# Turning layer-norm rows back to feature-major on VectorE and ScalarE instead of TensorE

## The chip, the cores and the metric

One core of a Trainium2 chip runs the whole program. The metric is the device time of one execution in microseconds; a change is judged by the ratio of the two kernels' times.

## The reference

For each of B = 8 samples `x` is 512 tokens by 256 features. Two residual blocks follow one another:

```python
# block 1, "context"
ctx = causal_ema(x, tau_ctx)
gated = x * sigmoid(concat(x, ctx) @ Wg.T + bg)
h1 = gelu(x @ Wn1.T + bn1); mod = 0.5 + sigmoid(h1 @ Wn2.T + bn2)      # D = 8 channels
temporal = sum_d softmax(blend)[d] * causal_ema(gated * mod[d], tau[d])
gate = sigmoid(temporal @ Wtemp.T + btemp); soma = gelu(x @ Wsoma.T + bsoma)
out = (soma * gate) @ Wout.T
x2 = x + (out - mean(out)) / sqrt(var(out) + 1e-5) * gamma + beta     # over the 256 features
# block 2, "experts": three shared FFNs and two that the sample's type picks, 256 -> 1024 (relu) -> 256
out = x2 + g0 * (wa * expert_a(x2) + wb * expert_b(x2)) + g1 * s0(x2) + g2 * s1(x2) + g3 * s2(x2)
```

The four gates `g` are a softmax made from the FFNs' outputs at token 0.

## The kernel before

Everything but the layer norm is held feature-major: partition = feature (two tiles of 128, index `c`), free = 512 tokens. To keep fp32 precision each operand is split into a rounded "hi" part (ScalarE) and a remainder "lo" (VectorE), and each product is three fp32r matmuls.

The expert pass of sample `b` is 40 slots (`SLOTS`): five FFNs of eight 128-wide hidden tiles. In slot `k` TensorE does `up` for hidden tile `k + 2` (LAG = 2), six matmuls into one of four banks `ps_up`, then `down` for tile `k`, six matmuls that accumulate into the two banks `ps_down`. ScalarE makes `hid_hi` by a relu (L1065), VectorE `hid_lo` (L1306, `relu_lo`); TensorE's down waits for both. When an FFN's eight tiles are done, ScalarE copies `ps_down` to `y` (`read_out`, L1078), and the first down of the next FFN waits for it at L723. In each engine's own program `read_out` of FFN 3 stands at slot 32, ahead of that slot's relu:

```python
def mixture(b, k, parity, last):          # ScalarE
    if k % TPF == 0 and 0 < k < SLOTS:
        read_out(b, k // TPF - 1, parity)
    if k + LAG < (LAST_SLOTS if last else SLOTS):
        relu(b, k + LAG, last)
```

While the experts of sample `b` run, the context block of sample `n = b + 1` is computed beside them ("context period" n, n = 1 to 7; sample 0's is an opening of its own). Which step of it stands where is written out by hand: a plan for each engine maps a slot to step names. A whole-numbered slot's steps are issued before that slot's expert work, those of a half-numbered one behind it. `PLANS` holds for n = 3 to 7, `FIRST_PLANS` for n = 1, where the FFN weights are split as well, and `SECOND_PLANS` for n = 2: the same plan one slot later from slot 20 on (VectorE from 11.5 on). Each engine runs its list strictly in order; a semaphore wait holds all that is behind it.

The steps around the change, with their slots in `PLANS`: TensorE `out` (28.5) multiplies token tiles, so that the result has tokens on the partitions, in `ps_aux`; VectorE `ln_stats` (29); ScalarE `ln_sqrt` (29.5); VectorE `ln_norm` (30) writes `normed` (128 tokens x 256 features, four token tiles, L1485); TensorE `turn` (32) transposes it back, eight 128x128 transposes into `ps_aux` (L848); ScalarE `turn` (33) applies gamma and beta on the way out (L1143); VectorE `x2` (33.5) adds x (L1494); `x2_hi` (34.5), `x2_lo` (35) split it for the next sample's up products, which begin at slot 38. In slot 31 VectorE also has the gate part of sample b, one L1341 and five L1344 behind its `relu_lo`. In the period n = 2 the turn is at 33 (TensorE) and 34 (ScalarE).

Of the kernel before, what the change touches and what calls it, by code (L numbers as in the profile page):

```python
# [7 lines left out]
ALU = mybir.AluOpType  # L8
ACT = mybir.ActivationFunctionType
# [24 lines left out]
TT = T // P  # L34
# [11 lines left out]

PLAN_TENSOR = {
    0.5: ["mod_hidden"], 1.5: ["soma"], 2.5: ["mod", "gate_hidden"], 4.5: ["wgate"],
    25.5: ["tgate"], 28.5: ["out"], 32: ["turn"],
}  # L50
PLAN_SCALAR = {
    1: ["mod_hidden", "gate_part_hi"], 2: ["soma"], 3: ["mod"], 4: ["gate_exp"], 5.5: ["wgate"],
    24.5: ["temp_hi"], 26: ["tgate"], 27: ["sg_hi"], 29.5: ["ln_sqrt"], 33: ["turn"], 34.5: ["x2_hi"],
    36: ["next_x_hi"],
}
PLAN_VECTOR = {
    0.5: ["gate_part"], 1.5: ["mod_hidden_lo"], 2: ["gate_part_lo"], 3.5: ["gate_logits"],
    4.5: ["gate_soft", "mix1"], 5: ["wgate_scan"], 5.5: ["mix2", "mix3"], 6: ["gated"], 6.5: ["mix0"],
    24.5: ["temp_lo"], 26.5: ["sg"], 27: ["sg_lo"], 29: ["ln_stats"], 30: ["ln_norm"], 33.5: ["x2"], 35: ["x2_lo"],
    36.5: ["next_x_lo"],  # L60
}
for _d in range(D):
# [8 lines left out]
def from_slot(plan, first, head):  # L71
# [99 lines left out]
def build(nc, x, w_ctx, params, types_row, types_all, shared_wi, shared_wo, expert_wi, expert_wo,  # L171
# [6 lines left out]
    with ExitStack() as ctx:  # L178
# [3 lines left out]
        def sem(name):  # L182
            return ctx.enter_context(nc.semaphore(name))
# [18 lines left out]
        x2 = sb("x2", [P, 2, CT, T])  # L202
# [19 lines left out]
        soma = sb("soma", [P, CT, T])  # L222
        gates = sb("gates", [P, CT, T])
# [5 lines left out]
        normed = sb("normed", [P, TT, E])  # L229
        ident = sb("ident", [P, P])  # L230
# [56 lines left out]
        aux_ready = sems("aux_ready", 2)  # L287
# [133 lines left out]
        def col(c, i=0):  # L421
            return par[:, c + i:c + i + 1]
# [232 lines left out]
        def _(pe):  # L655
# [122 lines left out]
            def beside(step, k, p):  # L778
# [45 lines left out]
                elif step == "out":  # L824

                    pe.wait_ge(sg_hi_ready, n)
                    places = [(t, c, slice(t * P, (t + 1) * P), slice(W_OUT + c * E, W_OUT + (c + 1) * E))
                              for t in range(TT) for c in range(CT)]
                    for t, c, tok, at in places:
                        if t % 2 == 0 and c == 0 and later(p.aux[t // 2]["out"]):  # L830
                            pe.wait_ge(aux_free[t // 2], p.aux[t // 2]["out"])
                        place = ps_aux[t // 2][:, (t % 2) * E:(t % 2 + 1) * E]
                        pe.matmul(place, xg_hi[:, c, tok], wc_hi[:, at], start=t % 2 == 0 and c == 0, stop=False)  # L833
                        pe.matmul(place, xg_hi[:, c, tok], wc_lo[:, at], start=False, stop=False)  # L834
                    pe.wait_ge(sg_split, n)
# [189 lines left out]
        def _(act):  # L1025
# [72 lines left out]
            def beside(step, k, p):  # L1098
# [35 lines left out]
                elif step == "ln_sqrt":  # L1134
                    act.wait_ge(meanvar_ready, n)
                    act.activation(std[:, :], meanvar[:, :, 1], ACT.Sqrt, bias=eps[:, :]).then_inc(std_ready, 1)
                elif step == "turn":

                    if later((n - 1) * 16):
                        act.wait_ge(out_stored, (n - 1) * 16)  # L1140
                    for c in range(CT):
                        act.wait_ge(aux_ready[c], p.aux[c]["turn"] + 1)
                        act.activation(x2[:, p.n_parity, c, :], ps_aux[c][:, :], ACT.Identity, bias=col(C_BETA, c),  # L1143
                                       scale=col(C_GAMMA, c)).then_inc(aux_free[c], 1)
                elif step == "x2_hi":
                    act.wait_ge(x2_ready, n * 2 + 2)
                    hi(both(x2_hi[:, p.n_parity, :, :]), both(x2[:, p.n_parity, :, :])).then_inc(x2_hi_ready, 1)
# [147 lines left out]
        def _(dve):  # L1295
# [124 lines left out]
            def beside(step, k, p):  # L1420
# [59 lines left out]
                elif step == "ln_norm":  # L1480
# [384 lines left out]
```

## Time and profile before

| | |
|---|---|
| runs | median 1045.18 us, 1044.25 to 1045.28, three runs |
| profiled execution | span 1044.1 us from the first to the last instruction; no other time of its own is given |
| TensorE busy | 1036.7 us (99%) |
| VectorE busy | 756.8 us (72%) |
| ScalarE busy | 405.0 us (39%) |
| GpSimd busy | 16.3 us (2%) |

Read it so: with TensorE at 99%, what counts is what its queue holds and whether it ever has to wait; the other engines' shares say how much room there is on average, not whether an instruction comes in time.

### The profile page before, as it was taken

The page shows a single profiled execution, that of the slowest core. Times are in us where ns is not written, and L with a number is a line of the kernel's source. Part 1 is how long each engine was busy: PE and PEld are TensorE (multiplying, and loading weights), DVE is VectorE, ACT ScalarE, POOL GpSimd, SP SyncE. Part 2 cuts the span into 40 slices and gives each one's busy share as a digit, 9 for nine tenths or more (in the row PEclk, how much of TensorE's full clock was granted, in tenths as well). Part 3 has the DMA queues.
Part 4 walks back from the last instruction along what each step waited for, and adds up shares of the span by engine and source line. Part 5 has one row for each costly group of instructions (what it writes and reads, how often), then busy time and mean ns, then how long its engine had stood idle before and what let it go on. Part 6 is the DMA issues. An engine that isn't in the chain of part 4 may idle for free.

```text
span 1044.1 us, 12751 instructions
## 1 busy us (share of the span) xinstructions
PE 1036.7 (99%) x4850; PEld 861.1 (82%) x4850; DVE 756.8 (72%) x1260; ACT 405.0 (39%) x663; POOL 16.3 (2%) x26
## 2 busy tenths in 40 slices
PE   8999999999999999999999999999999999999998
PEld 5688888888888888888888888888888888888898
DVE  6989977799547986389764996559955599545236
ACT  8654555423443234422344223433334432423232
POOL 1200000000000000000000000000000000000000
PEclk9999999999999999999999999999999999999999
DMA  5388999786354754466544664546645465355582
GB/s 213 121 313 275 312 356 356 282 324 240 131 192 167 257 181 162 162 238 210 197 164 163 231 235 152 185 162 242 208 154 201 163 235 204 146 201 191 203 323 90
DMA packets 38302, 223.02 MB, mean 214 GB/s; under 512 B 4514, under 2 KB 5282, under 8 KB 16610
## 3 DMA queue, kind: packets, MB, share of 16 engines
q1 hardware_dynamic: 35938, 209.63, 56.1%
q0 software_dynamic: 2304, 12.58, 3.2%
q8 instruction: 38, 0.62, 0.2%
q14 instruction: 22, 0.18, 0.0%
HBM read 188.51 MB, written 33.69 MB: 213 GB/s over the span
## 4 chain that ended last, share of the span: by engine, by line
PE 96%; DMA 2%; DVE 2%; issue 0%; SPq 0%; ACT 0%; DVEq 0%
PE ps_up L665 14%; PE ps_up L695 14%; PE ps_up L696 14%; PE ps_down L737 14%; PE ps_down L741 14%; PE ps_down L738 14%; PE ps_aux L658 2%; PE ps_aux L659 2%; PE ps_aux L660 2%; DMA wi<-split_wi 1%; DVE y L1633 1%; PE ps_aux L837 1%; PE ps_aux L834 1%; PE ps_aux L833 1%; PE ps_aux L822 1%; PE ps_aux L818 1%
## 5 line engine op out<-in xcount | busy, mean ns | idle before, releaser
L1065 ACT ACTIVATE hid_hi<-ps_up 128x512 fp32r<-128x512 f32 (+1 forms) x336 | 193.5, 576 | 507.8 <-PE ps_up L665 507.6
L1306 DVE SCALAR_TENSOR_TENSOR hid_lo<-ps_up,hid_hi 128x512 fp32r<-128x512 f32 (+1 forms) x336 | 220.1, 658 | 228.9 <-ACT hid_hi L1065 227.5
L695 PE MATMUL ps_up<-x_hi_all,wi 128*128 128x512 f32 (+1 forms) x660 | 250.8, 382 | 0.4 <-DMA wi<-split_wi 0.4
L696 PE MATMUL ps_up<-x_hi_all,wi 128*128 128x512 f32 (+1 forms) x660 | 249.9, 380 | 0.0
L737 PE MATMUL ps_down<-hid_hi,wo 128*128 128x512 f32 (+1 forms) x640 | 245.3, 384 | 0.1
L738 PE MATMUL ps_down<-hid_hi,wo 128*128 128x512 f32 (+1 forms) x640 | 245.1, 384 | 0.0
L665 PE MATMUL ps_up<-x_lo_all,wi 128*128 128x512 f32 (+1 forms) x660 | 197.4, 380 | 0.2 <-DVE x_lo_all L1297 0.2
L741 PE MATMUL ps_down<-hid_lo,wo 128*128 128x512 f32 (+1 forms) x640 | 193.9, 384 | 0.0
L695 PEld LDWEIGHTS ps_up<-x_hi_all,wi 128*128 128x128 f32 x660 | 124.1, 188 | 24.1 <-DMA wi<-split_wi 0.8
L696 PEld LDWEIGHTS ps_up<-x_hi_all,wi 128*128 128x128 f32 x660 | 124.1, 188 | 23.0
L665 PEld LDWEIGHTS ps_up<-x_lo_all,wi 128*128 128x128 f32 x660 | 122.0, 188 | 24.3 <-DVE x_lo_all L1297 0.4
L737 PEld LDWEIGHTS ps_down<-hid_hi,wo 128*128 128x128 f32 x640 | 120.2, 188 | 24.7 <-issue 0.2
L738 PEld LDWEIGHTS ps_down<-hid_hi,wo 128*128 128x128 f32 x640 | 120.2, 188 | 23.5
L741 PEld LDWEIGHTS ps_down<-hid_lo,wo 128*128 128x128 f32 x640 | 119.0, 188 | 24.0 <-DVE hid_lo L1306 0.3
L1416 DVE TENSOR_TENSOR_SCAN trace<-alpha,trace 128x512 f32<-128x512 f32 x98 | 119.1, 1216 | 0.0
L1450 DVE SCALAR_TENSOR_TENSOR trace<-modb,blend_w,gates 128x512 f32<-128x512 f32 x98 | 68.9, 744 | 0.0
L1459 DVE TENSOR_TENSOR temporal<-trace,temporal 128x512 f32<-128x512 f32 x98 | 62.1, 676 | 0.0
L1373 DVE SCALAR_TENSOR_TENSOR x<-y,g,x 128x512 f32<-128x512 f32 x56 | 38.9, 746 | 0.2
L658 PE MATMUL ps_aux<-xg_hi_all,wc_hi 128*128 128x512 f32 x88 | 34.5, 392 | 0.0
L659 PE MATMUL ps_aux<-xg_lo_all,wc_hi 128*128 128x512 f32 x88 | 34.3, 389 | 0.0
L660 PE MATMUL ps_aux<-xg_hi_all,wc_lo 128*128 128x512 f32 x88 | 34.2, 389 | 0.0
L1078 ACT ACTIVATE y<-ps_down 128x512 f32<-128x512 f32 x48 | 26.1, 596 | 18.5 <-PE ps_down L741 18.5
(248 smaller groups left out, 855.1 us busy)
## 6 DMA issues: line engine op xcount, KB each, us to landing
wi<-split_wi SPq DMA_DIRECT2D x70, 1024.0 KB, 4.8
wo<-split_wo SPq DMA_DIRECT2D x70, 1024.0 KB, 4.9
modb<-mod_scratch SPq DMA_DIRECT2D x28, 512.0 KB, 4.6
split_wi<-wi SPq DMA_DIRECT2D x10, 1024.0 KB, 7.3
split_wo<-wo SPq DMA_DIRECT2D x10, 1024.0 KB, 7.6
xt<-in_x SPq DMA_DIRECT2D x8, 512.0 KB, 5.8
split_wi<-ex POOLq DMA_DIRECT2D x4, 1024.0 KB, 8.6
split_wo<-ex POOLq DMA_DIRECT2D x4, 1024.0 KB, 6.0
```

The source lines that it names most:

```text
L658: pe.matmul(ps, w_hi, x_hi, start=start, stop=False)
L665: mm = pe.matmul(ps, w_hi[c], x2_lo[:, parity, c, tokens], start=False, stop=c == CT - 1)
L695: pe.matmul(ps, w_hi, x2_hi[:, parity, c, tokens], start=c == 0, stop=False)
L696: pe.matmul(ps, w_lo, x2_hi[:, parity, c, tokens], start=False, stop=False)
L737: pe.matmul(bank, w_hi[:, cols], hid_hi[:, at % NU, tokens], start=start, stop=False)
L738: pe.matmul(bank, w_lo[:, cols], hid_hi[:, at % NU, tokens], start=False, stop=False)
L741: mm = pe.matmul(bank, w, hid_lo[:, at % NU, tokens], start=False, stop=stop)
L1065: act.activation(hid_hi[:, k % NU, tokens], ps_up[k % NU][:, tokens], ACT.Relu).then_inc(hid_hi_ready, 1)
L1306: dve.scalar_tensor_tensor(hid_lo[:, k % NU, tokens], ps_up[k % NU][:, tokens], 0.0, f32(hid_hi[:, k % NU, tokens]), ALU.max, ALU.subtract ...
L1416: scan = dve.tensor_tensor_scan(trace_of(d)[:, c, :], alpha[:, d:d + 1].broadcast_to([P, T]), trace_of(d)[:, c, :], 0.0, ALU.mult, ALU.add)
L1450: dve.scalar_tensor_tensor(trace_of(d)[:, c, :], modb[:, d // 2 % 2, d % 2, :], blend_w[:, c, d:d + 1], gates[:, c, :], ALU.mult, ALU.mult ...
L1459: dve.tensor_tensor(temporal[:, c, :], trace[:, c, :], temporal[:, c, :], ALU.add).then_inc(ema_sum, 1)
```

## The change

`normed` is turned back without TensorE. VectorE's new step `turn` transposes each 32x32 block in place in the 128x256 tile (four instructions) into `gates`. A block's rows and columns are then right, but it may lie in the wrong partition quarter. ScalarE moves the blocks: step `turn<b>`, b = 0 to 3, has four copies of 32 partitions x 256 elements from quarter a of `gates` to quarter b of `soma`. Residual and beta are put into `x2` by ScalarE beforehand (`base`, slot 20.5), and VectorE's `x2` step multiplies by gamma and adds.

```diff
 PLAN_TENSOR:  ... 28.5: ["out"]
-    32: ["turn"]
 PLAN_SCALAR:
-    33: ["turn"]
+    20.5: ["base"], 31: ["turn0"], 31.5: ["turn1"], 32.5: ["turn2"], 33: ["turn3"]
 PLAN_VECTOR:
+    30.5: ["turn"]
 FIRST_PLANS:
-    "tensor": 33.5: ["turn"];  "scalar": 34.5: ["turn"]
+    "scalar": 21.5: ["base"], 32.5: ["turn0"], 33: ["turn1"], 33.5: ["turn2"], 34.5: ["turn3"];  "vector": 32: ["turn"]
...
+        turned_in_place = gates[:, :, :].rearrange("p c t -> p (c t)").rearrange("p (t c b j) -> p b c t j", t=TT, c=CT, b=4)
+        turned = soma[:, :, :].rearrange("p c (t a j) -> p a c t j", t=TT, a=4)
...
-                elif step == "turn":                                    # TensorE
-                    pe.wait_ge(normed_ready, n)
-                    for c in range(CT):
-                        for t in range(TT):
-                            mm = pe.transpose(ps_aux[c][:, t * P:(t + 1) * P], normed[:, t, c * P:(c + 1) * P], ident[:, :])
-                        mm.then_inc(aux_ready[c], 1)
...
-                elif step == "turn":                                    # ScalarE
+                elif step == "base":
                     if later((n - 1) * 16):
                         act.wait_ge(out_stored, (n - 1) * 16)
                     for c in range(CT):
-                        act.wait_ge(aux_ready[c], p.aux[c]["turn"] + 1)
-                        act.activation(x2[:, p.n_parity, c, :], ps_aux[c][:, :], ACT.Identity, bias=col(C_BETA, c),
-                                       scale=col(C_GAMMA, c)).then_inc(aux_free[c], 1)
+                        act.activation(x2[:, p.n_parity, c, :], x_of(n)[:, c, :], ACT.Identity, bias=col(C_BETA, c))\
+                            .then_inc(base_ready, 1)
+                elif step.startswith("turn"):
+                    b = int(step[-1])
+                    act.wait_ge(blocks_turned, n * TT)
+                    for a in range(4):
+                        hi(turned[quarter(b), a], turned_in_place[quarter(a), b]).then_inc(quarter_moved, 1)
...
+                elif step == "turn":                                    # VectorE
+                    dve.wait_ge(sg_split, n)
+                    for t in range(TT):
+                        dve.wait_ge(aux_free[t // 2], p.aux[t // 2]["out"] + 1)
+                        dve.transpose(gates[:, t // 2, (t % 2) * E:(t % 2 + 1) * E], normed[:, t, :]).then_inc(blocks_turned, 1)
                 elif step == "x2":
+                    dve.wait_ge(quarter_moved, n * 16)
+                    dve.wait_ge(base_ready, n * CT)
                     for c in range(CT):
-                        dve.wait_ge(aux_free[c], p.aux[c]["turn"] + 1)
-                        dve.tensor_tensor(x2[:, p.n_parity, c, :], x2[:, p.n_parity, c, :], x_of(n)[:, c, :], ALU.add)
+                        dve.scalar_tensor_tensor(x2[:, p.n_parity, c, :], soma[:, c, :], col(C_GAMMA, c),
+                                                 x2[:, p.n_parity, c, :], ALU.mult, ALU.add).then_inc(x2_ready, 1)
```

## Rows read from the trace of the kernel before

**Rows 1.** The page: busy time by engine; the chain that ended last

```profile
PE 1036.7 (99%) x4850; PEld 861.1 (82%) x4850; DVE 756.8 (72%) x1260; ACT 405.0 (39%) x663; POOL 16.3 (2%) x26
...
PE 96%; DMA 2%; DVE 2%; issue 0%; SPq 0%; ACT 0%; DVEq 0%
```

**Rows 2.** Groups by line and shape: busy us, mean ns | idle before

```profile
L1485 DVE TENSOR_SCALAR normed<-ps_aux,meanvar,rstd 128x256 f32<-128x256 f32 x28 | 13.3, 537 | 0.3
...
L1143 ACT ACTIVATE x<-ps_aux,par 128x512 f32<-128x512 f32 x14 | 10.1, 778 | 0.0
...
L1078 ACT ACTIVATE y<-ps_down,wa_now 128x512 f32<-128x512 f32 x14 | 8.9, 685 | 4.8 <-PE ps_down L741 4.8
...
L848 PE MATMUL ps_aux<-ident,normed 128*128 128x128 f32 x56 | 7.3, 272 | 0.0
...
L1224 ACT ACTIVATE modb<-ps_aux,gw 128x256 f32<-128x256 f32 x16 | 6.3, 528 | 0.0
...
L1027 ACT ACTIVATE modh_hi<-modh 128x512 fp32r<-128x512 f32 x7 | 4.4, 633 | 0.2
L1118 ACT ACTIVATE normed<-normed 8x512 f32<-8x512 f32 x7 | 4.4, 631 | 0.2
...
L871 PEld LDWEIGHTS ps_down<-ones_r 128*128 128x128 f32 x18 | 3.9, 331 | 1.3 <-DVE ones_r L1553 1.3
...
L893 PEld LDWEIGHTS ps_down<-y,gw 128*128 128x128 f32 x16 | 3.0, 190 | 3.9 <-issue 3.6 <-ACT gw L1190 0.2
...
L1027 ACT ACTIVATE ct_hi<-gpart 128x256 fp32r<-128x256 f32 x7 | 2.8, 403 | 1.7 <-DVE gpart L1506 1.7
```

**Rows 3.** Timeline of TensorE, slots 31 to 33, period n = 7: start, length

```profile
905.06 0.39 PE L695 MATMUL ps_up<-x_hi_all,wi 128*128 128x512 f32 x1
...
907.78 1.03 PE L848 MATMUL ps_aux<-ident,normed 128*128 128x128 f32 x8
908.57 0.48 PE L695 MATMUL ps_up<-x_hi_all,wi 128*128 128x512 f32 x1
...
910.03 0.39 PE L737 MATMUL ps_down<-hid_hi,wo 128*128 128x512 f32 x1
...
911.39 0.39 PE L695 MATMUL ps_up<-x_hi_all,wi 128*128 128x512 f32 x1
```

**Rows 4.** Timeline of ScalarE, the read of FFN 3, period n = 7

```profile
907.98 1.27 ACT L1078 ACTIVATE y<-ps_down,wa_now 128x512 f32<-128x512 f32 x2 [0.77 <-PE ps_down L741]
```

**Rows 5.** Timeline of VectorE, slots 30 and 31, period n = 7

```profile
903.63 1.90 DVE L1485 TENSOR_SCALAR normed<-ps_aux,meanvar,rstd 128x256 f32<-128x256 f32 x4
905.68 0.69 DVE L1306 SCALAR_TENSOR_TENSOR hid_lo<-ps_up,hid_hi 128x512 fp32r<-128x512 f32 x1
907.25 0.69 DVE L1306 SCALAR_TENSOR_TENSOR hid_lo<-ps_up,hid_hi 128x512 fp32r<-128x512 f32 x1 [0.88 <-ACT hid_hi L1065]
907.86 0.34 DVE L1341 TENSOR_SCALAR gpart<-gw,y 128x256 f32<-128x256 f32 x1
```

**Rows 6.** Timeline of ScalarE, a 128x256 copy and its follower

```profile
181.99 0.40 ACT L1027 ACTIVATE ct_hi<-gpart 128x256 fp32r<-128x256 f32 x1
182.29 0.58 ACT L1065 ACTIVATE hid_hi<-ps_up 128x512 fp32r<-128x512 f32 x1
```

**Rows 7.** Timeline of ScalarE at slot 21, period n = 7

```profile
873.80 0.60 ACT L1065 ACTIVATE hid_hi<-ps_up 128x512 fp32r<-128x512 f32 x1 [2.12 <-PE ps_up L665]
```

**Rows 8.** Timeline, period n = 2: TensorE's down(32), VectorE behind the gate part

```profile
281.00 0.39 PE L737 MATMUL ps_down<-hid_hi,wo 128*128 128x512 f32 x1
...
283.73 0.68 DVE L1306 SCALAR_TENSOR_TENSOR hid_lo<-ps_up,hid_hi 128x512 fp32r<-128x512 f32 x1
```

**Rows 9.** Timeline, period n = 1: VectorE's norm, TensorE's down(35)

```profile
155.40 1.90 DVE L1485 TENSOR_SCALAR normed<-ps_aux,meanvar,rstd 128x256 f32<-128x256 f32 x4
...
163.82 0.39 PE L737 MATMUL ps_down<-hid_hi,wo 128*128 128x512 f32 x1
```

**Rows 10.** Windows: length, PE, PEld, DVE, ACT, POOL busy, clock, DMA share, GB/s

```profile
0.00:3.00 3.00, 1.70 (x8) 1.70 (x9) 0.39 (x7) 1.34 (x2) 0.20 (x4) 1.00 0.20 34
```

More of the change, by code:

```diff
@@ L48 @@
     0.5: ["mod_hidden"], 1.5: ["soma"], 2.5: ["mod", "gate_hidden"], 4.5: ["wgate"],
-    25.5: ["tgate"], 28.5: ["out"], 32: ["turn"],
+    25.5: ["tgate"], 28.5: ["out"],
 }
@@ L52 @@
     1: ["mod_hidden", "gate_part_hi"], 2: ["soma"], 3: ["mod"], 4: ["gate_exp"], 5.5: ["wgate"],
-    24.5: ["temp_hi"], 26: ["tgate"], 27: ["sg_hi"], 29.5: ["ln_sqrt"], 33: ["turn"], 34.5: ["x2_hi"],
+    20.5: ["base"], 24.5: ["temp_hi"], 26: ["tgate"], 27: ["sg_hi"], 29.5: ["ln_sqrt"], 31: ["turn0"], 31.5: ["turn1"], 32.5: ["turn2"],
+    33: ["turn3"], 34.5: ["x2_hi"],
     36: ["next_x_hi"],
@@ L58 @@
     4.5: ["gate_soft", "mix1"], 5: ["wgate_scan"], 5.5: ["mix2", "mix3"], 6: ["gated"], 6.5: ["mix0"],
-    24.5: ["temp_lo"], 26.5: ["sg"], 27: ["sg_lo"], 29: ["ln_stats"], 30: ["ln_norm"], 33.5: ["x2"], 35: ["x2_lo"],
+    24.5: ["temp_lo"], 26.5: ["sg"], 27: ["sg_lo"], 29: ["ln_stats"], 30: ["ln_norm"], 30.5: ["turn"], 33.5: ["x2"], 35: ["x2_lo"],
     36.5: ["next_x_lo"],
@@ L79 @@
     "sync": from_slot(PLAN_SYNC, 8, {1: ["mod"], 1.5: ["modb0", "modb1"]}),
-    "tensor": {0.5: ["mod"], 1.5: ["wgate"], 27.5: ["tgate"], 30: ["out"], 33.5: ["turn"]},
-    "scalar": {0.5: ["mod"], 2: ["wgate"], 26: ["temp_hi"], 28: ["tgate"], 29: ["sg_hi"],
-               31: ["ln_sqrt"], 34.5: ["turn"], 35.5: ["x2_hi"], 37: ["next_x_hi"]},
+    "tensor": {0.5: ["mod"], 1.5: ["wgate"], 27.5: ["tgate"], 30: ["out"]},
+    "scalar": {0.5: ["mod"], 2: ["wgate"], 21.5: ["base"], 26: ["temp_hi"], 28: ["tgate"], 29: ["sg_hi"],
+               31: ["ln_sqrt"], 32.5: ["turn0"], 33: ["turn1"], 33.5: ["turn2"], 34.5: ["turn3"], 35.5: ["x2_hi"], 37: ["next_x_hi"]},
     "vector": {2: ["wgate_scan", "gated"],
-               26: ["temp_lo"], 28.5: ["sg"], 29: ["sg_lo"], 30.5: ["ln_stats"], 31.5: ["ln_norm"], 35: ["x2"], 36: ["x2_lo"],
+               26: ["temp_lo"], 28.5: ["sg"], 29: ["sg_lo"], 30.5: ["ln_stats"], 31.5: ["ln_norm"], 32: ["turn"], 35: ["x2"], 36: ["x2_lo"],
                37.5: ["next_x_lo"]},
@@ L313, in build @@
         rstd_ready = sem("rstd_ready")
-        normed_ready = sem("normed_ready")
-        turned_ready = sem("turned_ready")
+        blocks_turned = sem("blocks_turned")
+        base_ready = sem("base_ready")
+        quarter_moved = sem("quarter_moved")
         x2_ready = sem("x2_ready")
@@ L409, in build, with quarter @@
         open_total_of = open_traces[3]
+        turned_in_place = gates[:, :, :].rearrange("p c t -> p (c t)").rearrange("p (t c b j) -> p b c t j", t=TT, c=CT, b=4)
+        turned = soma[:, :, :].rearrange("p c (t a j) -> p a c t j", t=TT, a=4)
         def x_of(n):
             return xt[n % 2][:, :, :]
+        def quarter(i):
+            return slice(i * P // 4, (i + 1) * P // 4)
         def raw_part(i):
@@ L840, in beside @@
                             mm.then_inc(aux_ready[t // 2], 1)
-                elif step == "turn":
-                    pe.wait_ge(normed_ready, n)
-                    for c in range(CT):
-                        if later(p.aux[c]["turn"]):
-                            pe.wait_ge(aux_free[c], p.aux[c]["turn"])
-                        for t in range(TT):
-                            mm = pe.transpose(ps_aux[c][:, t * P:(t + 1) * P], normed[:, t, c * P:(c + 1) * P], ident[:, :])
-                        mm.then_inc(aux_ready[c], 1)
                 elif step == "gate_hidden":
@@ L1488, in beside @@
                             last.then_inc(aux_free[t // 2], 1)
-                    dve.wait_ge(aux_free[1], p.aux[1]["out"] + 1)
-                    dve.nop().then_inc(normed_ready, 1)
+                elif step == "turn":
[3 more added lines that the diff above has]
+                        dve.transpose(gates[:, t // 2, (t % 2) * E:(t % 2 + 1) * E], normed[:, t, :]).then_inc(blocks_turned, 1)
                 elif step == "x2":
+                    dve.wait_ge(quarter_moved, n * 16)
+                    dve.wait_ge(base_ready, n * CT)
                     for c in range(CT):
-                        dve.wait_ge(aux_free[c], p.aux[c]["turn"] + 1)
-                        dve.tensor_tensor(x2[:, p.n_parity, c, :], x2[:, p.n_parity, c, :], x_of(n)[:, c, :], ALU.add)\
-                            .then_inc(x2_ready, 1)
+                        dve.scalar_tensor_tensor(x2[:, p.n_parity, c, :], soma[:, c, :], col(C_GAMMA, c),
+                                                 x2[:, p.n_parity, c, :], ALU.mult, ALU.add).then_inc(x2_ready, 1)
                 elif step == "x2_lo":
```

## The prediction

> **What bounds the kernel.** I read the page first: TensorE is busy 99% of the span and holds 96% of the chain that ended last [rows 1]. A microsecond taken off TensorE's queue is therefore a microsecond off the end, and one in which it stands still is added. Then the grouped rows of the instructions that the change touches [rows 2], and the timelines of the three engines at the place of the change. The profiled span is 1044.1 us; the runs' median, 1045.18, is 1.1 us more, which I take as what lies around the span and leave alone.
>
> A slot of the expert pass is one "up" product (six matmuls) and one "down" product (six), 2.72 us. In the seventh context period slot 31 opens at 905.06, the eight transposes start at 907.78, slot 32's up at 908.57 and its down at 910.03 [rows 3]. What bounds slot 32's down is more than its weights: it opens the fifth FFN, and L723 makes it wait until ScalarE has read the fourth FFN out of the same bank (y, L1078). In the profile this is just in time: that read runs from 907.98 [rows 4], done for the first bank near 908.66, for the second near 909.25.
>
> **What the change takes off TensorE.** From slot 31's start, 905.06, to slot 32's start, 908.57, is 3.51 us, 0.79 over the 2.72 of a plain slot; from there to the slot after (911.39) is 2.82, 0.10 over it [rows 3]. Eight transposes cost 0.89 us, in seven periods 6.2 us. The 273 ns of one matmul times 56 would give 15 us, but they overlap [rows 2], so the spacing counts. If nothing else happened the time would be 1045.2 - 6.2 = 1039.0.
>
> **What it adds elsewhere.** VectorE: four 128x256 block transposes per period. No row shows one. Cheapest neighbour: a tensor_scalar of this shape in SBUF, 0.34 us; dearest: the one that writes normed, 537 ns, four in 1.90 us, so 454 ns apart [rows 2, 5]. Back-to-back VectorE instructions start some 75 ns before the last ends (0.69 long, the next 0.61 behind it [rows 5]), so 0.27 apart at the low end. I take 0.35 apart and 0.42 for the last, between the ends: four in 1.47 us (low 1.15, high 1.89).
> ScalarE: sixteen copies of 32 partitions x 256 elements. Nearest row: the 128x256 copy in SBUF, 403 ns on average; where a relu follows at once, it starts 0.30 later [rows 2, 6]. That a quarter of the partitions makes a copy cheaper isn't to be expected: a copy of 512 elements takes 0.63 us on 8 partitions and on 128 [rows 2]. I take 0.31 apart (low 0.30, high 0.40, no overlap). The Trainium skill (ScalarE: Activation LUTs, What ACT_TABLE_LOAD costs) gives 186 ns + 0.833 ns an element, with 93 ns of overlap; by it a copy is 0.40 and 0.306 apart, and the sum would stay.
> "base" is two activations at slot 20.5, at most as long as the two that go away at slot 33 (0.78 [rows 2]), in a ScalarE that rests 2.12 us between relus there [rows 7]: nothing.  The x2 step takes 0.75 instead of 0.68 twice, on VectorE, nothing: its consumer, TensorE at slot 38, is some 8 us later. No DMA is moved.
>
> **Where it lands.** This is the step that decides. Both engines take their work in the order in which the plan lists it. ScalarE's order in the third to seventh period is: relu(32); turn0 (waits for all four transposes, four copies); relu(33); turn1 (four copies); then, at slot 32, the read of the fourth FFN; relu(34); turn2; turn3. So that read, for which TensorE waits, now stands behind the wait for VectorE and eight copies.
> Seventh period: VectorE finishes the norm at 905.53 and has relu_lo(32) at 905.68, after which the next can start at 906.29 [rows 5]. Transposes end at 906.29 + 1.47 = 907.76. ScalarE, with 0.04 for the semaphore: 907.80 + 8 x 0.31 + 0.50 (relu(33) in series) = 910.78, where the read begins; its first bank is ready 0.68 later (685 ns [rows 2]), 911.46. TensorE would want it at 910.03 - 0.89 = 909.14. Wait 2.32, and 0.13 more because the second bank comes 0.58 after the first while TensorE wants it 0.45 after: 2.45. Less the 0.89, the period loses 1.56 us. The offsets from the norm to TensorE's transposes are the same in periods three to seven (4.15 us from 903.63 to 907.78 here), so 5 x 1.56 = 7.8. Low: 5 x 1.16 = 5.8. High (transposes to 908.18, read from 911.92): 5 x 2.70 = 13.5.
> Second period: its plan is one slot later from 11.5 (VectorE) and 20 (ScalarE) on, so only turn0 stands ahead of the read, but the transposes, at 31.5, stand behind slot 31's gate part: VectorE is at relu_lo(33), a 0.34 and five gate products until 283.73, where the transposes can start [rows 8]. They end at 285.20; turn0 4 x 0.31, the read's first bank 0.68: 287.16. TensorE starts slot 32's down at 281.00 in the profile, its transposes come a slot later, so nothing has been saved yet: wait 6.16 + 0.13 = 6.29, loss 5.40 (low 5.04, high 6.18).
> First period: its turn0 comes at 32.5, after the read, so no read is held. What is queued behind the copies is relu(35): the norm ends at 157.30 [rows 9], transposes 158.77, eight copies and a relu 161.9; TensorE's down(35) wants it at 163.82 - 0.89 = 162.9. In time. relu(36), behind a splitting round, turn2: 164.6 against 165.65. Gain 0.89, at the high costs nothing (0.1 and then 0.5 late, and the copies' other followers).
> Sum: -0.9 + 5.4 + 7.8 = +12.3 us (low 10.0, high 19.7).
> After the waits nothing else is late: in periods three to seven turn3 ends near 915, x2 and its halves are ready by 920, and slot 38 isn't before 925. relu_lo(33) and the gate part slide behind the late relu(33) to about 913.5, and relu_lo(34) is wanted after 917.
>
> **The clock.** The granted TensorE clock is 1.00 (2.4 GHz) even in the first 3 us, which hold the longest idle stretch of TensorE, 1.3 us [rows 2, 10]. Yet after its idle start the first 18 weight loads (fp32) take 331 ns against 190 for later ones of that type, 2.5 us lost in all [rows 2, 10]. A 6.3 us wait may cost that again: 0 to 2.6, I take 1.3. So +13.6: 1044.1 + 13.6 = 1057.7 in the span, **1058.8 us** by the runs. The Trainium skill (TensorE: Matmul & The Clock Gate, Why this matters for your kernels) says that a long idle gap between matmuls sends the array back to half clock; the granted clock here has not yet shown it.
> The same skill's VectorE: DVE Perf Modes (Rules for kernel authors) says to give a 128x128 transpose to TensorE where PSUM will do as its destination, and by its table the VectorE one is the shorter (311 against 390 ns). Here neither figure decides; the queue does.
>
> **Rivals.**
> Only the saving shows (1039.0): the quarter copies would have to be so cheap that the read isn't late: it must start by 908.42, which leaves 1.6 us for four transposes and eight copies after 906.29; a copy's time doesn't fall with its partitions, by the rows above. And with copies at nothing the second period still waits for the transposes until 284.9 at best, 4.7 us with the read: -6.2 + 4.7 = -1.5, 1043.7, no change that could be told. So below 1043 is possible only if TensorE doesn't wait for that read. Chances 2% faster, 2% for 1043.7.
> Each wait costs the clock: 2.6 us at all six instead of 1.3 at one, 1073. For: the opening's slow loads. Against: a wait of 2.4 us isn't one of 6, and the granted clock at the slow loads is 1.00 too, so that they may have another cause [rows 10]. The skill's rule above would be this one, if 2.4 us counted as long. 9%.
> Both operations dearer: transposes at twice 0.454 = 0.91 apart, copies at 0.53 (the 128x256 activation out of PSUM at L1224 [rows 2], no overlap): the period waits 906.29 + 3.6 + 0.04 + 4.2 + 0.5 + 0.7 - 909.14 = 6.2, loss 5.4, times 5 = 27; the second 8.4; the first some 3: 1084. For: no row has either operation, both read or write in runs of 32 elements. 7%.
>
> **Numbers.** The sum as worked out has 80%, its own range 1055 to 1067.5 (10.0; 19.7 + 2.6). For 8 in 10 I take 1054 to 1070. What a measurement of this kernel can tell from no change is 0.2%, 2.1 us. Faster 2%, same 2%, slower 96%.
>
> **What would show it.** ScalarE's L1078 after "turn1" by about 2.8 us in periods three to seven, TensorE idle before L737 of slot 32, released by y, 2 to 3.5 us five times and about 6 us once, none in the first; the four block transposes near 0.42 us and the sixteen copies near 0.40. I'm wrong if L1078 isn't waited for, if the transposes are done long before 907.8, or if the copies on 32 partitions are far from 0.3 apart.

## The result and the profile after

The changed kernel takes 1081.17 us (1080.19 to 1081.94, four runs) against 1045.03 (1044.25 to 1045.28, four runs): ratio 1.0344, 95% interval [1.0329, 1.0358]. The direction was forecast, the size was not: 36 us slower, where I gave 14 and a range up to 25.

The page, busy time by engine, the chain that ended last, and two groups (answering to [rows 1]):

```profile
PE 1044.7 (97%) x4794; PEld 862.5 (80%) x4794; DVE 765.8 (71%) x1288; ACT 449.8 (42%) x775; POOL 16.3 (2%) x26
...
PE 89%; DVE 3%; ACT 3%; DMA 2%; issue 2%; SPq 0%; POOL 0%; DVEq 0%; POOLq 0%; ACTq 0%
...
L745 PE MATMUL ps_down<-hid_hi,wo 128*128 128x512 f32 (+1 forms) x640 | 248.3, 389 | 23.0 <-ACT y L1077 21.5
...
L1026 ACT ACTIVATE soma<-gates 32x256 f32<-32x256 f32 x112 | 46.4, 414 | 24.6 <-DVE gates L1497 22.1
```

TensorE has 56 instructions less and is busy 8 us longer. ScalarE waits 22.1 us for the block transposes, and TensorE 21.5 us for ScalarE's read-out of `ps_down` (L1077 now, L1078 before). The view of who waited for whom, TensorE alone (us in total, times, longest):

```profile
PE ps_down L745 <- ACT y L1077: 21.5, 6, 6.4
PE ps_aux L666 <- ACT modh L1109: 3.9, 1, 3.9
...
PE ps_down L745 <- DVE y L1330: 0.9, 1, 0.9
...
PE ps_down L745 <- ACT hid_hi L1064: 0.6, 1, 0.6
```

Six waits for the read, one in each of the periods 2 to 7, as forecast. The other three lie in the first period, and none of them was there before. Waits explain some 27 us; the rest is slow work behind them, shown next. The seventh period, timelines of ScalarE, VectorE and TensorE (start, length), answering to [rows 3 to 5]:

```profile
938.26 1.74 ACT L1026 ACTIVATE soma<-gates 32x256 f32<-32x256 f32 x4 [3.00 <-DVE gates L1497]
939.90 0.57 ACT L1064 ACTIVATE hid_hi<-ps_up 128x512 fp32r<-128x512 f32 x1
940.50 1.73 ACT L1026 ACTIVATE soma<-gates 32x256 f32<-32x256 f32 x4
942.25 1.27 ACT L1077 ACTIVATE y<-ps_down,wa_now 128x512 f32<-128x512 f32 x2
```

```profile
936.21 0.68 DVE L1310 SCALAR_TENSOR_TENSOR hid_lo<-ps_up,hid_hi 128x512 fp32r<-128x512 f32 x1
936.81 1.42 DVE L1497 STREAM_TRANSPOSE gates<-normed 128x256 f32<-128x256 f32 x4
```

```profile
939.45 0.61 PE L673 MATMUL ps_up<-x_lo_all,wi 128*128 128x512 f32 x2
943.08 0.47 PE L745 MATMUL ps_down<-hid_hi,wo 128*128 128x512 f32 x1 [3.02 <-ACT y L1077]
...
945.40 0.63 PE L703 MATMUL ps_up<-x_hi_all,wi 128*128 128x512 f32 x1
...
947.55 0.40 PE L745 MATMUL ps_down<-hid_hi,wo 128*128 128x512 f32 x1
```

The order on ScalarE is the one of the prediction: wait for the transposes, four copies, a relu, four copies, and only then the read. Slot 32's down starts at 943.08; a start-to-start spacing of 0.23 behind the up product's last matmul would have been 939.90: 3.18 us lost. Then down and the next up take 2.32 and 2.15 us instead of 1.36 each. The windows say why (length, busy time of PE, PEld, DVE, ACT, POOL, granted clock, DMA share, GB/s):

```profile
938.00:941.00 3.00, 2.06 (x10) 1.37 (x8) 0.72 (x2) 2.62 (x7) 0.00 (x0) 1.00 0.38 117
941.00:944.00 3.00, 0.92 (x3) 0.73 (x4) 2.82 (x7) 2.93 (x6) 0.00 (x0) 0.94 0.55 232
944.00:947.00 3.00, 3.00 (x8) 2.33 (x8) 0.73 (x2) 2.83 (x8) 0.00 (x0) 0.50 0.00 0
947.00:950.00 3.00, 3.00 (x14) 2.41 (x14) 1.62 (x3) 1.08 (x3) 0.00 (x0) 0.99 0.37 101
```

After the wait the granted clock is 0.50 (1.2 instead of 2.4 GHz) for some 3.4 us: eight matmuls in 3 us instead of fourteen. That costs 0.96 in the down product, 0.79 in the up product and 0.03 behind them, 1.78 us. 3.18 + 1.78 - 0.89 saved = 4.07, and the period is 4.0 longer.

The second period, VectorE, ScalarE and TensorE, answering to [rows 8]:

```profile
290.81 1.42 DVE L1497 STREAM_TRANSPOSE gates<-normed 128x256 f32<-128x256 f32 x4
```

```profile
292.27 1.73 ACT L1026 ACTIVATE soma<-gates 32x256 f32<-32x256 f32 x4 [5.87 <-DVE gates L1497]
294.02 1.26 ACT L1077 ACTIVATE y<-ps_down,wa_now 128x512 f32<-128x512 f32 x2
```

```profile
294.85 0.76 PE L745 MATMUL ps_down<-hid_hi,wo 128*128 128x512 f32 x1 [6.37 <-ACT y L1077]
```

The first period, ScalarE, GpSimd and TensorE, answering to [rows 9]; behind them two windows:

```profile
158.06 3.50 ACT L1026 ACTIVATE soma<-gates 32x256 f32<-32x256 f32 x8 [1.20 <-DVE gates L1497]
161.58 0.60 ACT L1064 ACTIVATE hid_hi<-ps_up 128x512 fp32r<-128x512 f32 x1
...
185.05 1.06 ACT L1026 ACTIVATE ex<-ex 128x1024 fp32r<-128x1024 f32 x1 [6.96 <-DMA ex<-in_expert_wo]
186.13 1.28 ACT L1109 ACT_TABLE_LOAD   x1
187.42 0.69 ACT L1109 ACTIVATE modh<-ps_aux,par 128x512 f32<-128x512 f32 x1
```

```profile
165.87 0.54 POOL L1785 DMA_DIRECT2D split_wi<-ex  x1 [14.41 <-DVE ex L1301]
...
177.95 0.53 POOL L1777 DMA_DIRECT2D ex<-in_expert_wo  x1 [9.00 <-DMA split_wi<-ex]
```

```profile
165.79 0.47 PE L745 MATMUL ps_down<-hid_hi,wo 128*128 128x512 f32 x1 [0.56 <-ACT hid_hi L1064]
178.40 0.47 PE L745 MATMUL ps_down<-hid_hi,wo 128*128 128x512 f32 x1 [0.94 <-DVE y L1330]
188.16 0.50 PE L666 MATMUL ps_aux<-xg_hi_all,wc_hi 128*128 128x512 f32 x1 [3.92 <-ACT modh L1109]
```

```profile
185.00:188.00 3.00, 0.00 (x0) 0.00 (x0) 0.00 (x0) 2.92 (x3) 0.00 (x0) 1.00 0.97 397
188.00:191.00 3.00, 2.84 (x9) 2.28 (x10) 1.41 (x2) 2.97 (x6) 0.00 (x0) 0.72 0.15 61
```

In this pass the expert weights are split as well, a tile at a time: GpSimd loads a tile, ScalarE and VectorE split it, GpSimd stores it and loads the next into its place. The eight copies put relu(35) at 161.58, where it was at 157.68 before; VectorE's remainder of the tile stands behind relu_lo(35) and came 3.9 us later (163.95 instead of 160.05). The store went out at 165.87 instead of 161.98, into a stretch (170 to 182) in which the transfers fill 0.97 to 1.00 of the DMA engines, as they do at the same place before, and the next tile's load at 177.95 instead of 170.62. ScalarE asks for that tile at slot 40 and stands 7 us before it, with the next period's Gelu behind it, and TensorE 3.9 us for the Gelu, with the clock down after it. An operation that is 4 us late came back as a hole 25 us later. (The times of before are its own timelines' starts of the same instructions. The changed kernel's opening is 0.6 us shorter, so against the start of the period each of them is 0.6 later still.)

The whole difference by periods, measured from the start of one period's reciprocal of the norm to the next one's, so that each length holds one turn:

| kernel | period 1 | 2 | 3 to 6, each | 7 to the end |
|---|---|---|---|---|
| before | 122.81 | 122.93 | 125.62 | 140.7 |
| after | 130.74 | 130.35 | 129.63 | 144.8 |
| difference | +7.9 | +7.4 | +4.0 | +4.1 |

7.9 + 7.4 + 4 x 4.0 + 4.1 = 35.4; the opening was 0.6 shorter; the spans differ by 34.9 (1079.0 to 1044.1).

### The profile page after: what moved, and what is told of

It is laid out like the page before. It is cut to its first block, busy times and chain, and to the rows that moved or that the text cites. A ratio compares the mean times of both kernels' runs of the same rounds, so it can differ in the third digit from the quotient of the medians.

```text
span 1079.0 us, 12773 instructions
## 1 busy us (share of the span) xinstructions
PE 1044.7 (97%) x4794; PEld 862.5 (80%) x4794; DVE 765.8 (71%) x1288; ACT 449.8 (42%) x775; POOL 16.3 (2%) x26
## 4 chain that ended last, share of the span: by engine, by line
PE 89%; DVE 3%; ACT 3%; DMA 2%; issue 2%; SPq 0%; POOL 0%; DVEq 0%; POOLq 0%; ACTq 0%
PE ps_down L745 13%; PE ps_up L703 13%; PE ps_up L704 13%; PE ps_down L749 13%; PE ps_down L746 13%; PE ps_up L673 13%; PE ps_aux L666 2%; PE ps_aux L668 2%; PE ps_aux L667 2%; ACT soma L1026 2%; DMA wi<-split_wi 1%; DVE y L1641 1%; DMA ex<-in_expert_wo 1%; PE ps_aux L842 1%; PE ps_aux L845 1%
## 5 line engine op out<-in xcount | busy, mean ns | idle before, releaser
L745 PE MATMUL ps_down<-hid_hi,wo 128*128 128x512 f32 (+1 forms) x640 | 248.3, 389 | 23.0 <-ACT y L1077 21.5
L746 PE MATMUL ps_down<-hid_hi,wo 128*128 128x512 f32 (+1 forms) x640 | 247.7, 388 | 0.0
L749 PE MATMUL ps_down<-hid_lo,wo 128*128 128x512 f32 (+1 forms) x640 | 196.8, 389 | 0.0
L703 PEld LDWEIGHTS ps_up<-x_hi_all,wi 128*128 128x128 f32 x660 | 126.0, 191 | 25.6 <-DMA wi<-split_wi 1.1
L704 PEld LDWEIGHTS ps_up<-x_hi_all,wi 128*128 128x128 f32 x660 | 126.0, 191 | 23.8
L1026 ACT ACTIVATE soma<-gates 32x256 f32<-32x256 f32 x112 | 46.4, 414 | 24.6 <-DVE gates L1497 22.1
L667 PE MATMUL ps_aux<-xg_lo_all,wc_hi 128*128 128x512 f32 x88 | 34.9, 397 | 0.0
## 6 DMA issues: line engine op xcount, KB each, us to landing
split_wi<-ex POOLq DMA_DIRECT2D x4, 1024.0 KB, 10.5
```

Source lines behind the costliest of these rows:

```text
L703: pe.matmul(ps, w_hi, x2_hi[:, parity, c, tokens], start=c == 0, stop=False)
L704: pe.matmul(ps, w_lo, x2_hi[:, parity, c, tokens], start=False, stop=False)
L745: pe.matmul(bank, w_hi[:, cols], hid_hi[:, at % NU, tokens], start=start, stop=False)
L746: pe.matmul(bank, w_lo[:, cols], hid_hi[:, at % NU, tokens], start=False, stop=False)
L749: mm = pe.matmul(bank, w, hid_lo[:, at % NU, tokens], start=False, stop=stop)
L1026: return act.activation(out_ap, in_ap, ACT.Copy)
```

## The experiments

The theory after the result: (1) in periods 2 to 7 the read of FFN 3 stands behind the block copies in ScalarE's queue; (2) TensorE's wait brings down its clock, which costs 1.8 us more each time; (3) the first period's loss is the copies' place among the splitting work. Rivals: ScalarE has no room for the copies wherever they stand; the slow matmuls have another cause; the first period's loss is scatter of its transfers.

**e1: the turn steps behind the read, periods 2 to 7.**

```diff
 PLAN_SCALAR:
-    31: ["turn0"], 31.5: ["turn1"], 32.5: ["turn2"], 33: ["turn3"], 34.5: ["x2_hi"], 36: ["next_x_hi"]
+    32.5: ["turn0"], 33.5: ["turn1"], 34: ["turn2"], 34.5: ["turn3"], 35.5: ["x2_hi"], 36.5: ["next_x_hi"]
 PLAN_VECTOR:
-    33.5: ["x2"], 35: ["x2_lo"], 36.5: ["next_x_lo"]
+    35: ["x2"], 36: ["x2_lo"], 37: ["next_x_lo"]
```

> All four turn steps stand behind the read of FFN 3 in periods 2 to 7, the first period is left as changed. Theory (queue order: the read behind the copies, then the slow clock, makes the loss): periods 2 to 7 lose their waits and keep the saving of 0.89 us, so 7.4 + 0.9 in the second and 5 x (4.0 + 0.9) = 24.5 in the others come off 1081.2: 1048.4. Rival A (the copies take ScalarE's time wherever they stand, so relus come late instead): at least half of the loss stays, above 1062. Rival B (VectorE's and ScalarE's new work slows TensorE's own operand reads): no wait remains but the slots are longer than 2.72 us.

Measured: 1047.98 us (ratio to before 1.0023, [1.0014, 1.0033]), 0.4 from the theory's value. Period 2 is 122.27 and each of 3 to 6 is 124.7, 0.9 shorter than before; TensorE has no wait left there. The same sixteen copies, as long as before (0.416 us each), cost nothing when they stand one to two slots later. Period 1 is still 130.96, and the ten executions spread from 1044.19 to 1049.44. Part (1) is shown, and the removal is worth what it was priced at.

**e3: one step moved, for the price of a copy and of a short wait.**

```diff
 PLAN_SCALAR:
-    31: ["turn0"], 31.5: ["turn1"], 32.5: ["turn2"],
+    31: ["turn0"], 32.5: ["turn1", "turn2"],
```

> Only turn1 goes behind the read (to 32.5, before turn2), in periods 3 to 7; in the second period turn1 was behind it already. Theory: the wait falls by four copies, 1.74 us, from 3.2 to 1.4 us, and if so short a wait doesn't bring the clock down, 1.8 us more: 5 x 3.5 = 17.7 less than 1081.2, 1063.5. If the clock falls after 1.4 us as well: 5 x 1.74 = 8.7 less, 1072.5. Rival (the wait is for VectorE's transposes, not for the copies): the wait stays near 3, 1081.

Measured: 1063.33 us ([1.0166, 1.0197]). Its third period, TensorE, and two windows:

```profile
420.16 0.47 PE L745 MATMUL ps_down<-hid_hi,wo 128*128 128x512 f32 x1 [1.27 <-ACT y L1077]
```

```profile
418.00:421.00 3.00, 1.73 (x8) 1.01 (x8) 1.60 (x4) 2.95 (x6) 0.00 (x0) 1.00 0.77 281
421.00:424.00 3.00, 3.00 (x15) 2.45 (x14) 2.38 (x5) 2.83 (x8) 0.00 (x0) 1.00 0.17 68
```

Four copies less ahead of the read make the wait 1.27 instead of 3.02, and after it the granted clock stays 1.00. Both together are 3.3 us a period (126.3 instead of 129.6), nearly twice what the copies themselves take. In the profiled execution, the fastest of the four (span 1059.8), periods 3 to 7 give 16.5 us of the 17.7 expected, and the untouched first period 2.4, so part of how well the median fits is luck.

**e4: the wait kept, its idleness taken away.** TensorE gets matmuls whose result nobody reads.

```diff
+PLAN_TENSOR[32] = ["fill"]; SECOND_PLANS["tensor"][32] = ["fill"]
...
+                elif step == "fill":
+                    pe.wait_ge(aux_free[1], p.aux[1]["out"] + 1)
+                    for _ in range(26 if n == 2 else 12):
+                        pe.matmul(ps_aux[1][:, :], wc_hi[:, 0:P], x2_hi[:, 1 - p.n_parity, 0, :], start=True, stop=True)
```

> TensorE has matmuls without a use to do at slot 32 (12 of 512 columns in periods 3 to 7, 26 in the second) where it would wait. The read comes no earlier. Theory (part of the loss is the clock, which falls in the wait to the lower level): the granted clock stays at 1.00, 1.8 us a period are won in periods 3 to 7 and about 1.9 in the second, 5 x 1.8 + 1.9 = 11 less than 1081.2: 1070, though TensorE does more. Rival (the slow matmuls behind the wait have another cause, such as late operands): same or slower than 1081, 0.5 us in longer stretches of work.

Measured: 1069.72 us ([1.0220, 1.0251]). Periods 3 to 6 are 128.1 each, 1.5 shorter than in the changed kernel with 12 matmuls more, the second is 1.6 shorter, and the window behind the wait (the third period's) shows the clock at 1.00:

```profile
421.00:424.00 3.00, 3.00 (x13) 2.35 (x14) 1.54 (x3) 2.88 (x7) 0.00 (x0) 1.00 0.02 5
```

Part (2) is shown: the slow stretch belongs to the idleness, not to the read or the copies. What stays in 128.1 against 125.6 is the wait itself, less the saving. Of the 11.4 us between the two profiled spans, 9.4 lie in the periods 2 to 7; 2.4 lie in the first, which e4 doesn't touch (the opening gives 0.4 back), so the matmuls are worth 9.4 and not the whole difference, and that the median fits the 11 expected is in part luck.

**e5: the second period's transposes ahead of the gate part.**

```diff
+SECOND_PLANS["vector"][31] = ["ln_norm", "turn"]
+del SECOND_PLANS["vector"][31.5]
```

> In the second period alone VectorE's transposes go from slot 31.5 to 31, ahead of relu_lo(33) and the six instructions of the gate part. Theory: its wait of 6.4 us falls by what stood before them, 0.6 + 0.4 + 2.5 = 3.5 us, to some 2.9; the clock falls as well, but for a shorter stretch or as long: 1081.2 - 3.5 = 1077.7 (1076.5 to 1078). Rival (the second period waits longer because of its transfers or of the first period's delay): no change, 1081.

Measured: 1075.09 us ([1.0267, 1.0302]); the profiled execution, at a span of 1076.7, was nearer the changed kernel's 1079.0. The second period's wait is 2.90, as expected to 0.1, and the period 126.77 instead of 130.35: 3.6 less. So its long wait was VectorE's queue, not transfers. The median fell by 6.1, more than that; the first period, which scatters (below), has to hold the rest, but no row of mine shows it.

**e6: the tiles asked for later.**

```diff
-TILE_ROUNDS = {24: 0, 25: 1, 32: 2, 33: 3, 40: 4, 41: 5, 45: 6, 46: 7}
-TILE_RESTS = {26: 0, 27: 1, 33: 2, 34: 3, 41: 4, 42: 5, 46: 6, 47: 7}
+TILE_ROUNDS = {24: 0, 25: 1, 32: 2, 33: 3, 44: 4, 45: 5, 50: 6, 51: 7}
+TILE_RESTS = {26: 0, 27: 1, 33: 2, 34: 3, 45: 4, 46: 5, 51: 6, 52: 7}
```

> The splitting of the weight tiles 4 to 7 on ScalarE and VectorE goes 4 to 5 slots later, the rest is as changed. Theory for the first period: ScalarE waits 7 us for tile 4 with the Gelu of the next period behind it, TensorE waits 3.9 us for that Gelu and then has the lower clock; with the tile asked for later both go, 5 to 6 us of the 7.9: 1075.5. Rival (the Gelu is late for the copies themselves, not for the tile): still 1081.

Measured: 1079.31 us ([1.0309, 1.0343]), 1.9 less than the changed kernel where I expected 5 to 6. TensorE's wait for the Gelu is gone, but the first period is 128.24, and two other profiled kernels with its unchanged first plan had 128.35 (e3) and 128.36 (e4), against 130.74, 130.96 (e1) and 131.87 (e5). So the length of the period alone doesn't tell what the tile's wait is worth. The trace does, if one looks at the place. From the start of the down product ahead of the Gelu to the start of the up product behind it are 4.08 us in the kernel before (181.50 to 185.58), 9.78 in the changed one (182.72 to 192.50) and 4.08 again in e6 (183.00 to 187.08). The tile's wait with the slow clock behind it is worth 5.7 us, as expected. e6 loses most of it again 40 us later, where the splitting that was put off meets VectorE's other work:

```profile
238.16 0.30 PEld L749 LDWEIGHTS ps_down<-hid_lo,wo 128*128 128x128 f32 x2 [0.41 <-DVE hid_lo L1310]
```

A wait of 1.0 us for a hid_lo at 232 and 0.2 to 0.3 us in nearly every slot up to 268 add up to 4.1 us; VectorE is busy without a break from 235 to 265 there, in the kernel before only to 255. The same stretch tells what scatters in the first period: up to the Gelu all kernels with its unchanged plan are 1.83 us behind the kernel before; the stretch at the Gelu then takes 8.4 us in e3 and e4, 9.8 in the changed kernel and 10.5 to 10.7 in e1 and e5, by a wait of 2.5 to 3.9 us and a slow clock of 3.4 or 6.8 us. Why the tile lands at different times stays open.

**e2: the first period's turns spread as well.**

```diff
 FIRST_PLANS, on top of e1:
-    "scalar": 32.5: ["turn0"], 33: ["turn1"], 33.5: ["turn2"], 34.5: ["turn3"], 35.5: ["x2_hi"], 37: ["next_x_hi"]
+    "scalar": 33.5: ["turn0"], 34.5: ["turn1"], 35: ["turn2"], 35.5: ["turn3"], 36.5: ["x2_hi"], 37.5: ["next_x_hi"]
-    "vector": 35: ["x2"], 36: ["x2_lo"], 37.5: ["next_x_lo"]
+    "vector": 36: ["x2"], 37: ["x2_lo"], 38: ["next_x_lo"]
```

> As the kernel before this one, and in the first period too the turns are spread: slots 33.5, 34.5, 35, 35.5, x2 at 36. Theory: the first period's 7.9 us come from relu(35) behind eight copies, which makes VectorE's rest of a weight tile late, so it goes as well and only the saving of 7 x 0.89 = 6.2 us is left: 1038.8, faster than both kernels. Rival: the first period has no room for 7 us of copies on ScalarE at all, they are late wherever they stand: 1042 to 1048.

Measured: 1043.51 us ([0.9973, 0.9991]), which is in the rival's range (1042 to 1048) and 4.7 from the theory; period 1 is 126.77. But it was not the copies themselves that were late. A new wait had come in, VectorE's and TensorE's timelines:

```profile
168.07 2.57 DVE L1348 SCALAR_TENSOR_TENSOR gpart<-gw,y,gpart 128x256 f32<-128x256 f32 x5
170.55 1.22 DVE L1301 TENSOR_TENSOR x_lo_all<-x,x_hi_all 128x1024 fp32r<-128x1024 f32 x1
```

```profile
171.83 0.74 PE L673 MATMUL ps_up<-x_lo_all,wi 128*128 128x512 f32 x2 [2.31 <-DVE x_lo_all L1301]
```

x2's remainder stood behind the gate part at slot 36, and slot 38's up product waited for it.

**e8: the gate part behind it.**

```diff
 on top of e2:
-FIRST_GATE_PART_SLOT = 36
+FIRST_GATE_PART_SLOT = 38
```

> As e2_late_both, but in the first period VectorE's gate part goes from slot 36 to 38, behind the remainder of x2 (2.9 us of work that stood ahead of it in e2, where TensorE waited 2.3 us at slot 38 and then had the lower clock). Theory: this was all that was left of the first period's loss; no wait remains in the seven periods and the saving shows in full, 1045.1 - 6.2 = 1038.9 (1038 to 1040). Rival (the splitting pass with its transfers has no room for the copies): another wait takes its place, 1041 or more.

Measured: 1040.7 us, ratio 0.9956 ([0.9943, 0.9970]). That wait is gone, period 1 is 123.55. The median is 0.7 above the expected range and just under the rival's 1041: the period is still 0.7 above before where 0.9 below was expected. Two small waits are left in it:

```profile
177.20 0.47 PE L745 MATMUL ps_down<-hid_hi,wo 128*128 128x512 f32 x1 [0.36 <-DVE y L1330]
```

```profile
225.22 0.50 PE L703 MATMUL ps_up<-x_hi_all,wi 128*128 128x512 f32 x1 [0.64 <-DMA wi<-split_wi]
```

The second was 0.36 in the kernel before, so the two explain 0.6 of the 1.6 us; the rest lies in products that start a little late without a wait that the view names, and its cause is not shown.

**e9: TensorE turns in the first period, blocks in the others.**

```diff
 on top of e1, FIRST_PLANS:
+    "tensor": 33.5: ["pe_turn"];  "scalar": 34.5: ["pe_turn"]          # TensorE's and ScalarE's turn of the kernel before
-    "scalar": 21.5: ["base"], 32.5: ["turn0"], 33: ["turn1"], 33.5: ["turn2"], 34.5: ["turn3"];  "vector": 32: ["turn"]
```

> The first period turns on TensorE as the kernel before, periods 2 to 7 by blocks with all turn steps behind the read of FFN 3. Theory: the first period is 122.8 us again, periods 2 to 7 save 0.89 us each: 1045.1 - 5.3 = 1039.8. Rival (the first period's loss is noise of its transfers and not of the steps there): the same as e1, near 1048.

Measured: 1040.09 us, ratio 0.9950 ([0.9937, 0.9964]), 0.3 from the expectation; period 1 is 122.59, the others as in e1. With e1 and e8 this settles part (3): with only the first period's way of turning changed, 7.9 us go, so it isn't scatter of the transfers. e8 and e9 beat the kernel before by 0.4 and 0.5%, little but clear of the noise; e9's four best executions are below all of e8's, though the two ratios' intervals overlap.

**e7 and e10: what spaces the copies.** The changed kernel's copies last 0.414 us, as priced, but start 0.435 apart, with no overlap. In the two runs the turn steps have four other copies each (turn3 of e7 stays as it was). One execution each:

```diff
 e7
+ b == 0: hi(aside[:, a], turned_in_place[:, 0])                              # 128 partitions; aside: trace, same pattern
+ b == 1: hi(turned[quarter(1), a], turned_in_place[quarter(1), a])
+ b == 2: hi(soma[quarter(2), a // 2, ...], gates[quarter(a), a // 2, ...])   # 256 in a row
 e10
+ b == 0: hi(aside[quarter(1), a], turned_in_place[quarter(0), a])
+ b == 1: hi(turned[quarter(a), 1], turned_in_place[quarter(a), 1])
+ b == 2: hi(turned[quarter(a), 2], turned_in_place[quarter(2), a])
+ b == 3: hi(aside[2 * P // 4:P, a], turned_in_place[0:2 * P // 4, a])        # 64 partitions
```

> The quarter copies are replaced by others, so that the blocks are not moved to their places (output is not the reference's): turn0 has 128 partitions instead of 32 with the same pattern, none moved; turn1 32 partitions in their own quarter; turn2 32 partitions moved, contiguous 256 elements; turn3 as changed. Measured is the spacing of the four. Theory (moving to another quarter prevents the overlap of neighbours): turn0 and turn1 0.31 apart, turn2 and turn3 0.435. Rival 1 (32 partitions do): turn0 alone 0.31. Rival 2 (the broken-up pattern does): turn2 alone 0.31. Rival 3: all 0.435, it is the same in any copy whose semaphore is raised each time from SBUF to SBUF.

> The quarter copies are replaced by others (output is not the reference's). turn0: four copies from quarter 0 to quarter 1, the same two quarters each time; turn1: quarter a to quarter a, a different one each time; turn2: from quarter 2 to a different one each time; turn3: 64 partitions, lower half to upper half. Theory (it is the move to other partitions that costs the overlap of some 0.12 us): turn0 and turn3 0.435 apart, turn1 0.31, turn2 0.435 but for the one that isn't moved. Rival (it is the change of quarter from one instruction to the next): turn0 and turn3 0.31, turn1 and turn2 0.435.

ScalarE's timelines of the third period, e7, then e10 (the length is that of the whole group of four or eight):

```profile
417.54 1.34 ACT L1026 ACTIVATE trace<-gates 128x256 f32<-128x256 f32 x4 [3.00 <-DVE gates L1505]
...
419.38 1.33 ACT L1026 ACTIVATE soma<-gates 32x256 f32<-32x256 f32 x4
...
422.52 3.49 ACT L1026 ACTIVATE soma<-gates 32x256 f32<-32x256 f32 x8
```

```profile
420.02 1.34 ACT L1026 ACTIVATE trace<-gates 32x256 f32<-32x256 f32 x4 [3.00 <-DVE gates L1505]
...
421.87 1.71 ACT L1026 ACTIVATE soma<-gates 32x256 f32<-32x256 f32 x4
...
425.38 1.73 ACT L1026 ACTIVATE soma<-gates 32x256 f32<-32x256 f32 x4
427.14 1.34 ACT L1026 ACTIVATE trace<-gates 64x256 f32<-64x256 f32 x4
```

Four in 1.34 us are (1.34 - 0.41) / 3 = 0.31 apart, four in 1.73 are 0.44. After e7 my theory (the move to other partitions costs the overlap) still stood: turn0 and turn1, which don't move, are 0.31 apart, turn2 and turn3 0.44. e10 ends it: from quarter 0 to quarter 1 four times, and from the lower to the upper half, all 0.31; in place but in a different quarter each time, 0.43; from one quarter to changing ones 0.44. It is the change of partition quarter, of source or destination, from one instruction to the next, the rival of e10. In the change every copy has another source quarter than the one before.

The two traces also show what a wait between 1.3 and 3 us does. With the cheaper copies TensorE waits 2.23 us for the read in each of the periods 3 to 7 of e7, and 2.62 in each of e10. Windows behind the waits of the third and the fourth period, e7:

```profile
421.60:424.60 3.00, 3.00 (x13) 2.35 (x14) 1.87 (x4) 2.88 (x7) 0.00 (x0) 1.00 0.15 63
548.90:551.90 3.00, 3.00 (x9) 2.23 (x10) 1.83 (x4) 2.88 (x7) 0.00 (x0) 0.62 0.16 63
```

The same wait brought the clock down in one period and not in the other: in three of five in e7 and in three of five in e10. Where it fell, the period is 1.6 us longer (128.87 against 127.27 in e7).

## Why the prediction was wrong in size

The direction and the place of the waits were right. Three steps failed: the first period's "In time. Gain 0.89", the clock's "0 to 2.6, I take 1.3", and the copies' "I take 0.31 apart".

**The saving** of 0.89 us a period was right: periods 3 to 6 are 124.70 in e1, e8 and e9 against 125.62, the last is 0.9 shorter as well, the second 0.7 (122.27 against 122.93).

**The cause in periods 2 to 7** was right, place and order: the read behind VectorE's transposes and the copies, one wait in each, the second period's the longest because of the gate part. e1, e3 and e5 bear it out. Transposes: 1.42 us for four against 1.47 priced. The copies' duration was 0.414 against 0.40.

**"I take 0.31 apart"** was mis-sized: 0.435, above my own high end of 0.40. The full-partition row in [rows 6] didn't carry over, since the copies change quarter; the 0.306 that stands beside it in the prediction is met by the copies of e7 and e10 that stay in the same quarters (0.31) and by no others. The prediction had named copies far from 0.3 as a sign of being wrong. With it the wait was 3.18 instead of 2.45 in periods 3 to 7 (+0.7 each, 3.7 in all), and 0.2 more in the second.

**"0 to 2.6, I take 1.3"**, for the clock and for the long wait alone, was the largest miss. The clock falls after each wait of 3 us, and each fall costs about 1.8 us. From 5 x 1.78, and in the second period 7.4 + 0.9 - 6.5 (its start of down against the place in the profile before) = 1.8, it is 10.7, 9.4 more than taken. My rival "each wait costs the clock" had this mechanism at 2.6 a time and 1073 in all, at 9%. The ground on which I held it small, that 2.4 us isn't 6, was never a measurement. With copies 0.435 apart the waits were 3 us anyway, and e3 shows 1.27 as harmless. The forecast wait of 2.45 would not have been safe either: waits of 2.23 and 2.62, on either side of it, brought the clock down in six of ten periods (e7, e10). The rule of the Trainium skill that I cited beside it (TensorE: Matmul & The Clock Gate, Why this matters for your kernels) agrees with the windows at 0.50, half clock, behind the waits of 3 and 6.4 us.

**"First period: ... In time. Gain 0.89"** failed: +7.9 instead of -0.9, 8.8 us. I followed relu(35) and relu(36) to TensorE's need for them and stopped there. Not followed was VectorE behind the late relu: the tile's remainder, the store, the load into the same buffer, and ScalarE's next request for it. Even for the relus it was off by a little (relu(36) is waited for by 0.56, none forecast at my values), because of the spacing. Waits of 5.4 us and windows at 0.72 and 0.71 of the clock (1.7 us) make up 7.1; the remaining 1.6 to the 8.8 are shorter gaps. By place, 2.7 us of the 8.8 are lost before the Gelu, 5.8 at it and 0.3 later. e6, where the tile is asked for later and the stretch at the Gelu takes 4.08 us as before, shows that the chain over the tile is what costs 5.7 of it; e9 shows that the copies set it off.

Sum: 1058.8 + 8.8 + 3.7 + 0.2 + 9.4 = 1080.9, measured 1081.2. That it fits to 0.3 is in part chance: the 1.1 us "around the span" came from two different executions and is 1.6 wherever a run has both times, and the opening was 0.6 shorter, which no step of mine has.

**Open:** what makes the tile land at different times in the first period, by which that period scatters by 3.5 us; the last 1 us in e8's first period; and what decides whether a wait between 2.2 and 2.6 us brings the clock down.

## What to carry to other kernels

In engines that work in order, price new work by what stands behind it in the queue: here copies ahead of a read-out cost 4 to 7 us in each of the periods 2 to 7, and nothing a slot or two later. Follow a delay past the nearest consumer until a buffer is given back and loaded again, above all where the transfers are already at their limit. And a wait of the bounding TensorE isn't priced by its length alone: 1.3 us cost 1.3, 3.2 us cost 5, and between them, at 2.2 to 2.6, the 1.6 us on top come sometimes. When you judge an experiment by its median, look in the trace whether the periods that you didn't touch have stayed the same.

## What the runs showed of the hardware

The granted clock after each of TensorE's waits of 3.0 us was 0.50 for about 3.4 us before it came back, and for 3.7 us behind the end of the one of 6.4; after 1.27 us it stayed 1.00 each time (e3). After 2.23 and 2.62 us it fell in three periods of five (e7, e10), and after e2's 2.31 us it was 0.57 in the next 3 us. Doing useless matmuls in the wait kept it at 1.00 and made the periods 2 to 7 9.4 us shorter together (e4).

Back-to-back ScalarE copies of 256 elements start 0.31 us apart on 128, 64 or 32 partitions, moved or not, as long as the partition range stays the same from one to the next, and 0.43 to 0.44 where it changes, on either side.

VectorE's 32x32 block transpose of a 128x256 fp32 tile took 0.404 us, four in 1.42.
